# Attention and channel mixing in one kernel: more probability tiles transposed by block transposes and DMAs, the input normalised on GpSimd, and new timetables

## What is computed

```python
xn = layernorm(x)                                  # over the last axis
# attention: 8 query heads of 128, one shared key and value head
q = xn @ Wq + bq + pe;  k, v = split(xn @ Wkv + bkv);  k = k + pe
p = softmax(causal(q @ k.T / sqrt(128)))           # 1024 x 1024 for each head
attn = concat_heads(p @ v) @ Wo
# channel mixing, with the token before (zero for the first)
xr = mu_r * xn + (1 - mu_r) * prev(xn);  xk = mu_k * xn + (1 - mu_k) * prev(xn)
ffn = sigmoid(xr @ W_r) * (relu(xk @ W_k)**2 @ W_v)
out = x + attn + ffn
```

## Time and profile before

| | us |
|---|---|
| median of three runs (1562.58 to 1563.08) | 1562.81 |
| the profiled execution, whole | 1561.37 |
| its span, first to last instruction | 1559.6 |
| PE busy, 12032 matmuls | 1533.5 |
| VectorE, ScalarE, GpSimd busy | 1210.4, 1056.2, 1060.7 |
| mean granted clock of PE | 0.996 |

### The profile page before, as it was taken

The page is one execution under the profiler, slowest core; times in us unless marked ns, Lnnn a source line. Parts: engine busy times, 40 slices in busy tenths (PEclk is TensorE's granted clock), DMA queues, the critical chain, the costliest instruction groups (busy, mean ns, idle before and its releaser), DMA issues.

```text
span 1559.6 us, 35317 instructions
## 1 busy us (share of the span) xinstructions
PE 1533.5 (98%) x12032; PEld 1497.6 (96%) x12032; DVE 1210.4 (78%) x3284; ACT 1056.2 (68%) x2531; POOL 1060.7 (68%) x1549
## 2 busy tenths in 40 slices
PE   5999999999999999999999999999999999999998
PEld 5999999999999999999999999999999999999998
DVE  6888767887678876788768787688876888768875
ACT  5776667766667766677577676676766677666764
POOL 5666776667756777567775676756766577765765
PEclk8999999999999999999999999999999999999999
DMA  4014420244202441024410244103431034300443
GB/s 139 9 53 121 146 75 22 58 122 148 69 15 69 129 143 55 15 75 134 144 42 15 86 141 127 42 15 98 140 129 32 12 112 138 129 20 8 119 147 105
DMA packets 151425, 132.46 MB, mean 85 GB/s; under 512 B 12240, under 2 KB 146512, under 8 KB 151248
## 3 DMA queue, kind: packets, MB, share of 16 engines
q1 hardware_dynamic: 150672, 129.55, 27.0%
q10 hardware_dynamic: 576, 0.66, 0.1%
HBM read 67.25 MB, written 62.91 MB: 83 GB/s over the span
## 4 chain that ended last, share of the span: by engine, by line
PE 76%; POOL 10%; issue 7%; DVE 5%; ACT 1%; DMA 0%; POOLq 0%; DVEq 0%; ACTq 0%
PE pS L893 25%; PE pO L893 23%; PE pG L893 19%; PE pT L986 8%; POOL qt L450 3%; POOL X L506 3%; DVE gate L698 1%; POOL pt L465 1%; POOL mh L456 1%; DVE X L872 1%; POOL rstd L434 1%; DVE mix L742 1%; POOL v L444 1%; POOL X L505 1%; DVE pt L797 1%
## 5 line engine op out<-in xcount | busy, mean ns | idle before, releaser
L893 PE MATMUL pO<-pt,v 128*128 128x256 f32 x3456 | 466.6, 285 | 6.5 <-DVE ot L848 5.3
L893 PE MATMUL pS<-kt,qt 128*128 128x288 f32 (+41 forms) x2304 | 458.6, 329 | 2.0 <-POOL qt L450 2.0
L659 ACT ACTIVATE X<-X,bias 128x16 f32<-128x16 f32 (+56 forms) x512 | 375.9, 734 | 93.3 <-DVE bias L872 92.8
L893 PEld LDWEIGHTS pO<-pt,v 128*128 128x128 f32 x3456 | 426.1, 189 | 12.1 <-DVE ot L848 10.0
L872 DVE CUSTOM_DVE_ANT_0 X<-pS,mask 128x16 f32<-128x16 f32 (+56 forms) x512 | 353.8, 691 | 45.1 <-issue 22.9
L506 POOL TENSOR_SCALAR X<-X,rec 128x16 f32<-128x16 f32 (+56 forms) x512 | 367.0, 717 | 23.0 <-DVE rec L780 23.0
L893 PEld LDWEIGHTS pS<-kt,qt 128*128 128x128 f32 x2304 | 367.5, 190 | 14.0 <-issue 2.2
L465 POOL TENSOR_TENSOR pt<-Z,pt 128x640 fp32r<-128x640 f32 (+3 forms) x128 | 256.6, 2005 | 63.3 <-ACT pt L588 61.6
L797 DVE TENSOR_TENSOR pt<-pT,pt 128x512 fp32r<-128x512 f32 (+3 forms) x512 | 257.3, 522 | 26.6 <-ACT pt L595 23.7
L595 ACT CAST pt<-pT 128x512 fp32r<-128x512 f32 (+3 forms) x512 | 223.0, 461 | 61.7 <-PE pT L986 58.8
L652 ACT CAST ot<-pO 128x256 fp32r<-128x256 f32 x256 | 96.2, 376 | 241.2 <-PE pO L893 115.0
(11 more groups left out here) (101 smaller groups left out, 1788.6 us busy)
## 6 DMA issues: line engine op xcount, KB each, us to landing
park_dram<-Y SPq DMA_DIRECT2D x32, 512.0 KB, 2.6
Z<-park_dram SPq DMA_DIRECT2D x128, 128.0 KB, 2.8
park_dram<-Y SPq DMA_DIRECT2D x32, 448.0 KB, 3.0
Z<-park_dram SPq DMA_DIRECT2D x128, 112.0 KB, 2.5
park_dram<-Y SPq DMA_DIRECT2D x32, 384.0 KB, 2.9
Z<-park_dram SPq DMA_DIRECT2D x128, 96.0 KB, 2.3
park_dram<-Y SPq DMA_DIRECT2D x32, 320.0 KB, 2.7
Z<-park_dram SPq DMA_DIRECT2D x128, 80.0 KB, 2.1
```

Of the source, the lines that this page charges most:

```text
L659: nc.scalar.activation(x_row(s, 0, w), x_row(s, 0, w), ACT.Exp, bias=bias[:, j:j + 1], scale=-1.0, accum_out=total[:, j:j + 1]).then_inc(e ...
L893: last = nc.tensor.matmul(out, a[i], m[j], start=start and k == 0, stop=stop and k == n - 1)
```

## The change

It sets `turned` to the even steps from 16 on: the first step of each pair in rows 2 and 3 of tiles (3 and 4 key tiles) takes the detour too, 24 tiles of a batch row in place of 16. `Y` and `park_dram` get two and four slots, the fetch is split from `park` and issued one turn later, `park` and `fetch` stand ahead of the stores in SP's program. `xnt` and `xt` have one buffer, with waits on ScalarE (`xt_ready`, `prev_ready`, `mix_ready`) ahead of its reuse. `norm_apply` moves from VectorE to GpSimd. On PE, `WO` stands ahead of the other fillers and of the pair's product; on VectorE statistics and `token_mix` stand behind the fillers' evictions; on GpSimd `split_q` and `split_v` stand ahead of the side work. `LEAD` is 10; `TURNS`, `WO_AT`, `AT` and `HALVES` have new entries. The staging of the weights moves to other parts of `X` and `Y`. A path on which ScalarE scales (`scaled_by_act`) is never taken, as no step is over 999, and `H_LAG` for odd steps is not used either. The core of the diff (the other three chunks' entries in `TURNS` are changed in the same way: `FV` of chunks 1 and 2 goes from 12 to 14, `Q` of chunk 1 from 11 to 9, `KT` and `KV` one turn earlier, `FR` of chunk 3 from 5 to 7):

```diff
-H_LAG = 7
-L_LAG = 7
+H_LAG = (7, 6)
+L_LAG = (7, 7)
+C_LAG = 2
 QTMP = 2
-LEAD = 12
+LEAD = 10
...
      (7, "FR", 0, 0),
      (8, "Q", 1, 1),
      (10, "Q", 1, 2),
-     (12, "KV", 1, 0),
+     (11, "KV", 1, 0),
      (13, "Q", 1, 3),
      (14, "FV", 0, 0),
-     (15, "KT", 1, 0)),
+     (14, "KT", 1, 0)),
     ((0, "FK", 0, 0),
      (3, "XT", 1, 0),
      (4, "FR", 0, 0),
      (7, "Q", 1, 0),
      (8, "Q", 1, 1),
-     (11, "Q", 1, 2),
-     (12, "FV", 0, 0),
-     (12, "KV", 1, 0),
+     (9, "Q", 1, 2),
+     (11, "KV", 1, 0),
      (12, "Q", 1, 3),
-     (14, "KT", 1, 0)),
+     (13, "KT", 1, 0),
+     (14, "FV", 0, 0)),
...
-WO_AT = (17, 25, 33, 41, 49, 57, 66, 72)
+WO_AT = (17, 26, 33, 41, 49, 56, 65, 73)
 AT = {"stats": (0, 0, 0, 0),
       "apply": (0, 0, 0, 0),
       "inv": (0, 0, 0, 0),
-      "mixr_prev": (0, 1, 0, 0),
-      "mixr_dve": (1, 1, 1, 1),
+      "mixr_prev": (0, 0, 0, 0),
+      "mixr_dve": (0, 1, 1, 0),
       "mixr_out": (3, 2, 4, 1),
-      "ka_out": (6, 5, 6, 8),
-      "mixk_prev": (5, 7, 6, 7),
-      "mixk_dve": (6, 13, 9, 11),
-      "mixk_out": (8, 14, 13, 13)}
-HALVES = (0, 1, 2, 3, 6, 4, 0, 1, 2, 3, 5, 4, 0, 1, 6, 2, 3, 4, 0, 1, 5, 2, 3, 4, 6, 0, 1, 2, 3, 7, 8, 9)
+      "ka_out": (8, 5, 6, 8),
+      "mixk_prev": (5, 4, 6, 7),
+      "mixk_dve": (9, 12, 11, 10),
+      "mixk_out": (10, 14, 14, 13)}
+HALVES = (1, 7, 6, 9, 8, 5, 1, 7, 6, 9, 8, 5, 1, 7, 6, 9, 8, 5, 1, 7, 8, 9, 1, 5, 8, 7, 1, 9, 4, 6, 5, 8, 0, 2, 4, 6, 0, 8, 4, 2, 0, 6, 4, 8, 0, 2, 4, 6, 0, 8, 4, 2, 0, 6, 4, 8, 0, 2, 4, 6, 0, 8, 4, 2)
...
-    if s < SHARED:
-        return HALVES[s], 1
-    return (s // 2 % 2 * 2, 2) if turned(s) else ((s - SHARED) // 2 % 3 * 2 + 4, 2)
+    return HALVES[s], 1 if s < SHARED else 2
 
 
 def turned(s):
 
-    return s >= SHARED and s % 2 == 0
+    return s >= 16 and s % 2 == 0
+
+
+def zeroed(s):
...
+    return P - (s % H + 1) * SUB
+
+def scaled_by_act(s):
+    return s > 999
...
+        if it >= T_LAG and it - T_LAG < STEPS:
+            order += [(b, ("T", it - T_LAG, m)) for m in range(len(t_banks(it - T_LAG)))]
...
-        xnt = sb("xnt", [P, 2, CT, CHUNK + 1])
-        xt = [sb(f"xt{i}", [P, 2, CT, CHUNK], R) for i in range(2)]
+        xnt = sb("xnt", [P, CT, CHUNK + 1])
+        xt = [sb(f"xt{i}", [P, CT, CHUNK], R) for i in range(2)]
         qt = [sb(f"qt{i}", [P, 2, CHUNK // SUB, H, SUB], R) for i in range(2)]
...
-        Y = sb("Y", [P, 4, NT, 32])
+        Y = sb("Y", [P, 2, 4, NT, 32])
         Z = sb("Z", [P, 2, 4, NT, 32])
...
-            def move(b, s):
-
-                k = turned_no(b, s)
-                slot, nk = k % 2, s // H + 1
+            def park(b, s):
+
+                k, nk = turned_no(b, s), s // H + 1
                 sp.wait_ge(turned_ready, k + 1)
-                if k >= 2:
-                    sp.wait_ge(landed[slot], 64 * (k // 2))
-                sp.dma_start(park_d[slot, :, :, 0:nk * 32],
-                             Y[:, :, 0:nk, :].rearrange("p a k c -> p a (k c)")).then_inc(parked, 16)
+                if k >= 4:
+                    sp.wait_ge(landed[k % 4], 64 * (k // 4))
+                sp.dma_start(park_d[k % 4, :, :, 0:nk * 32],
+                             Y[:, k % 2, :, 0:nk, :].rearrange("p a k c -> p a (k c)")).then_inc(parked[k % 2], 16)
+
+            def fetch(b, s):
+
+                k, nk = turned_no(b, s), s // H + 1
+                sp.wait_ge(parked[k % 2], 16 * (k // 2 + 1))
                 if k >= 2:
                     sp.wait_ge(turned_lo, k - 1)
-                sp.wait_ge(parked, 16 * (k + 1))
                 for q in range(4):
-                    sp.dma_start(Z[32 * q:32 * (q + 1), slot, :, 0:nk, :].rearrange("r a k c -> r a (k c)"),
-                                 park_d[slot, :, q, 0:nk * 32].rearrange("(a r) n -> r a n", a=4)
-                                 ).then_inc(landed[slot], 16)
+                    sp.dma_start(Z[32 * q:32 * (q + 1), k % 2, :, 0:nk, :].rearrange("r a k c -> r a (k c)"),
+                                 park_d[k % 4, :, q, 0:nk * 32].rearrange("(a r) n -> r a n", a=4)
+                                 ).then_inc(landed[k % 4], 16)
 
             for b, it in turns():
+                if it - V_LAG - 1 in TURNED:
+                    fetch(b, it - V_LAG - 1)
+                if it - V_LAG in TURNED:
+                    park(b, it - V_LAG)
                 for r in [r for r in range(NT) if min(WO_AT[r] + 1, LAST_IT - 1) == it]:
                     store(b, r // TPC, r % TPC)
                 for r in [r for r in range(1, NT, TPC) if min(WO_AT[r] + 4, LAST_IT - 1) == it]:
                     if b < B - 1:
                         reload(b, r // TPC)
-                if it - V_LAG in TURNED:
-                    move(b, it - V_LAG)
...
+            def norm_apply(n, slot):
+                pool.wait_ge(rstd_ready, n + 1)
+                for t in range(TPC):
+                    nc.gpsimd.tensor_scalar(xn[:, t, :], xtok[:, slot, t, :], mv[:, t, 0:1], rstd[:, t:t + 1],
+                                            ALU.subtract, ALU.mult).then_inc(xn_ready, 1)
...
+                c, i = it // PER, it % PER
+                if it < STEPS:
+                    if i == AT["inv"][c] and not absent(b, c + 1):
+                        inv_std(chunk_no(b, c + 1))
+                    if i == AT["apply"][c] and not absent(b, c + 1):
+                        if chunk_no(b, c):
+                            pool.wait_ge(mixed, chunk_no(b, c))
+                        norm_apply(chunk_no(b, c + 1), (c + 1) % NC)
+                    if i == AT["mixr_out"][c]:
...
                 act.wait_ge(filled["XT"], n + 1)
+                if n:
+                    act.wait_ge(xt_ready, n)
+                    act.wait_ge(prev_ready, 2 * n * CT)
+                    act.wait_ge(mix_ready, 2 * n * CT)
                 g = g_bank("XT", c, 0).rearrange("p (t n) -> p t n", t=CT)
                 if c % NC:
-
-                    nc.scalar.copy(xnt[:, slot, :, 0:1], xnt[:, 1 - slot, :, CHUNK:CHUNK + 1])
-                nc.scalar.copy(xt[0][:, slot, :, :], g)
-                nc.scalar.copy(xnt[:, slot, :, 1:CHUNK + 1], g).then_inc(xnt_ready, 1)
+                    nc.scalar.copy(xnt[:, :, 0:1], xnt[:, :, CHUNK:CHUNK + 1]).then_inc(last_kept, 1)
+                nc.scalar.copy(xt[0][:, :, :], g)
+                if c % NC:
+                    act.wait_ge(last_kept, n - n // NC)
+                nc.scalar.copy(xnt[:, :, 1:CHUNK + 1], g).then_inc(xnt_ready, 1)
...
-                s = it - H_LAG
-                if s in TURNED:
+                for s in [s for s in TURNED if s + H_LAG[s % 2] == it]:
                     nk = s // H + 1
                     k = turned_no(b, s)
                     if b or s // 2 > 1:
                         act.wait_ge(pv_done, b * (STEPS // 2) + s // 2 - 1)
-                    act.wait_ge(landed[k % 2], 64 * (k // 2 + 1))
-                    nc.scalar.copy(pt_of(0, s, nk), Z[:, k % 2, :, 0:nk, :]).then_inc(turned_hi, 1)
+                    act.wait_ge(landed[k % 4], 64 * (k // 4 + 1))
+                    nc.scalar.copy(pt_of(0, s)[:, 0:nk, :].rearrange("p k (a c) -> p a k c", a=4),
+                                   Z[:, k % 2, :, 0:nk, :]).then_inc(turned_hi, 1)
...
                 dve.wait_ge(bn_done, n * 2 * TPC + TPC)
+                if n:
+                    dve.wait_ge(xn_ready, n * TPC)
                 dve.sem_inc(dve_passed, 1)
                 for t in range(TPC):
                     nc.vector.bn_aggr(mv[:, t, :], stats[:, t, :]).then_inc(bn_done, 1)
                 dve.wait_ge(bn_done, n * 2 * TPC + 2 * TPC)
                 nc.vector.tensor_scalar_add(vare[:, :], mv[:, :, 1], EPS).then_inc(var_ready, 1)
-
-            def norm_apply(n, slot):
-                dve.wait_ge(rstd_ready, n + 1)
-                for t in range(TPC):
-                    nc.vector.scalar_tensor_tensor(xn[:, t, :], xtok[:, slot, t, :], mv[:, t, 0:1],
-                                                   rstd[:, t:t + 1].broadcast_to((P, E)),
-                                                   ALU.subtract, ALU.mult).then_inc(xn_ready, 1)
...
-                    if k:
-                        dve.wait_ge(parked, 16 * k)
-                    nc.vector.transpose(Y[:, :, 0:nk, :].rearrange("p a k c -> p k a c"),
+                    if scaled_by_act(s):
+                        dve.wait_ge(scaled, b * C_FIRST[STEPS] + C_FIRST[s + 1])
+                    if k >= 2:
+                        dve.wait_ge(parked[k % 2], 16 * (k // 2))
+                    nc.vector.transpose(Y[:, k % 2, :, 0:nk, :].rearrange("p a k c -> p k a c"),
...
-                c, i = it // PER, it % PER
-                if it < STEPS:
-                    n = chunk_no(b, c)
-                    if i == AT["stats"][c] and not absent(b, c + 1):
-                        norm_stats(chunk_no(b, c + 1), (c + 1) % NC, b)
-                    if i == AT["apply"][c] and not absent(b, c + 1):
```

(23 more changed lines are left out.)

195 lines of the change are left out of this document (109 added, 86 removed).

## The result

The changed kernel is slower: median 1573.92 us of five runs (1571.56 to 1576.64) against 1562.81 (1562.34 to 1563.24) before; ratio 1.0074, 95% interval [1.0059, 1.0089]. I had forecast 1538.

What follows compares the result with a forecast made beforehand. PE's instruction stream, busy 98% of a 1559.6 us span, was taken as the bound. Less 19.0 (transposes) and 6 (normalisation) gave 1534.6; adding 1.8 around the span and 1.4 to the median gave 1538 us, range 1530 to 1553.

Steps and rivals of the forecast that it cites:

- Point 4: Normalised input moved from VectorE to GpSimd: VectorE earlier, PE's stalls for `ot` shrink; 6 us less, bounds 0 and 10.
- Point 1: 224 fewer transposes on PE, even steps 16 to 30: 19.0 us less, counting in full on the saturated stream.
- Point 2: Detour work on other engines: ScalarE and VectorE about unchanged, GpSimd's subtractions 78 us, under 80% busy, off the path.
- Point 3: Detoured tiles arrive before their product; tightest is step 16, 8.9 us needed of 9.9; cost 0, bound 6 us.
- The sign I named: For the detour's tiles arriving in time: no wait of ScalarE for `Z`, none of PE for GpSimd's `pt`.
- Point 5: Single buffer for `xnt` and `xt`, `WO` order, `LEAD`, `HALVES`, filler places: costed at 0, fillers +/- 4 us.
- (b): VectorE takes over as bound in steps 16 to 37, its block transposes waiting for scaling: 1545 to 1559, chance 0.2.
- the sign I gave for (b): PE waits of over 2 us a row whose releaser is VectorE's mask.
- (c): Slower: detour too long for rows 2 and 3, PE stands at each pair; 1576 us, chance 0.06.

Runs made afterwards that it cites:

- the microbenchmark: The kernel before with fourteen extra GpSimd operations at its start, 128x256 fp32, each form twice, each waiting for the one before; one run, 1571.17 us.
- the timetables alone: The changed kernel with normalisation back on VectorE and the detour from step 32 on only; new timetables, order and single buffers kept: 1559.48 us, 0.9984.
- the first experiment: The changed kernel with `norm_apply` back on VectorE in its old place, everything else as changed: 1560.44 us, 0.9992.

## Why the prediction was wrong

**Point 4 is the step that failed.** It priced the normalisation on GpSimd by its scaling of 272 elements, 0.49 us. That row is right: the same form takes 0.48 in the microbenchmark. But it is another pair of operations, and subtract with multiply takes 1.22. I had bounded the gain of this edit by 0 and 10 us, and put no upper end on the duration itself, though no row of before showed a subtract in such an instruction. The changed kernel against the one with one multiplication says what this was worth: 1.0074 - 0.9889 = 1.85%, 29 us, the clock that fell behind the stalls included. I had a sentence for what is queued behind ("the scaling of step 14 (30, 46, 62), one or two us late for a use four turns on"); that was the tile of an even step, and the same change makes VectorE's block transpose use it one turn on, at the head of an in-order queue. I had priced the two parts one by one, and the loss is where they meet.

**The gain of point 4 was real and too small.** With the old detour, from the timetables alone (1559.48) to a normalisation that VectorE doesn't stand for (1549.98, 1550.08), it is 9.5 us; I took 6, with 10 as the bound.

**Point 1 is wrong twice, in opposite directions.** A transpose is worth 0.11 us by the steps, 24.6 us for 224, and not 19.0: from the first transpose to the first start of the next work it is 0.24 us for three, but that next matmul starts 0.03 us behind the last transpose and the second one behind it comes 0.26 us later where 0.17 is the rule, and this 0.09 belongs to the group. And "lying on the saturated stream, it counts in full" is wrong: about 6 us arrive with both rows (1544.53 from 1549.98; 1543.31 from 1550.08), and 10.3 of 15.3 where no other work is moved. Row 2 brings 7 to 9 of its 96 x 0.11 = 10.5, row 3 nothing of its 128 x 0.11 = 14. The busy share of 98% and the few waits of the earlier trace rows don't show how closely the other engines follow PE: with both rows the table has 0.2 to 0.8 us given back at five steps of a row.

**Point 2** was right on ScalarE and VectorE (block transposes of 0.574 and 0.693 us in the first experiment), and too low on GpSimd only by the normalisation: 41.28 of 51.88 us in the third chunk are 80%.

**Point 3** was right by the medians and wrong for the tile that it named as the tightest. Writes of the tiles with 3 key tiles land after 2.4 us and fetches after 1.9 (below), where I took 2.7 and 2.1. But the write of step 16's tile landed after 4.0 to 4.3 us in five of the eight batch rows of the changed kernel, and in a sixth its fetches were issued late, and PE waited at the product of steps 16 and 17, as shown above: 4.5 us in all at step 24, where I took 0 and bounded it by 6. For the other new tiles it held: PE's one named wait for GpSimd's `pt`, 2.8 us in 7 cases, at most 0.4, is at the product of steps 62 and 63. The sign I named did appear, ScalarE waiting 26.0 us for `Z`; GpSimd's subtraction stands behind ScalarE's copy (72.6 us in all, 61.6 before).

```profile
park_dram<-Y SPq DMA_DIRECT2D x32, 192.0 KB, 2.4
Z<-park_dram SPq DMA_DIRECT2D x128, 48.0 KB, 1.9
```

**Point 5**, costed at 0, gave some 2.5 us (1 to 4 by the interval): the kernel with the timetables alone is at 0.9984.

**The sum again.** 1538, + 29 for the subtract, + 13 for transposes that don't arrive (6 in place of 19), - 6 for the larger gain of point 4 and the timetables, is 1574; measured 1573.9. It closes because each of these terms is a difference between runs; it is bookkeeping and no second proof.

**The rivals.** The mechanism of (b) is the one that came: a block transpose stands for GpSimd's scaling and holds what is behind it. I had put it at 0.75 us a stand, from 27.8 / 37, and let it end at 1559. The longest are 3.3 us, and PE met them at `WO`'s eviction, not at the mask, so the sign I gave for (b), a wait of over 2 us a row for the mask, didn't appear. The slower side, (c), was given 0.06 for a detour that is too long. It is too long for one tile, by 0.4 to 1.3 us in six batch rows, which doesn't make the kernel slower; no case had the normalisation in it.

**The shared interfaces.** I weighed the Trainium skill's rule (GPSIMD Engine Reference, Specifications: GpSimd's SBUF interfaces are shared with VectorE, and VectorE's instructions with two SBUF inputs or in a 2-port perf mode contend) at 4 us off the path. The last section shows that it holds here for `token_mix`, which has two SBUF inputs: 475 ns alone, 1180 beside `pt<-Z`. The normalisation behind the mask has one SBUF input besides its two pointers and lasts longer still, 1631; which mode it runs in, no trace shows. And it was not all off the path: turn 33, 1.0 us of VectorE's time in a row, and step 30, 0.3 us.

What stays open: why the write of one tile lands late in some batch rows, the rest of VectorE's 1.5 us before it normalises, and what lengthens step 38. That row 3 costs what it gives was measured.

## What to carry to other kernels

Price an operation on another engine by a row with the same operations, not only the same shape and name, and where no row has them give its duration an upper end and follow that end through the in-order queue behind it. Ask of every item in that queue who uses it after the change, since the same change may have moved the use closer. Look at single rounds of a loop beside the medians, since a tile that is late in half of them hides there, and look at the granted clock in each. On a stream that is 98% busy, work taken out counts in full only where the engines that take it over have slack in that very step, and a table of step lengths against a base shows where; move it tile by tile.

## What the runs showed of the hardware

GpSimd's `tensor_scalar` on 128x256 fp32 takes 0.40 to 0.56 us with multiplications and additions, and 1.07 to 1.22 us in the three forms whose first operation is a subtract, with constants as with pointers. The Trainium skill, GPSIMD Engine Reference, section "Elementwise — side-by-side cycle accounting", has 1.8 cycles an element at 1.2 GHz as the best case, an estimate of 0.38 us for 256 elements: the 0.40 us of two multiplications with constants agrees with it, and the 1.07 of the same with a subtract is nearly three times that. A subtraction written as mult and add with a negated, scaled shift is the way round, and costs two operations on 128x2 elements.

**VectorE beside GpSimd.** In the kernel that normalises behind the mask, the mean length of VectorE's instructions by what GpSimd did during the largest part of each (ns, number of cases):

| on VectorE | GpSimd idle | scaling of `X` | `pt<-Z` subtraction |
|---|---|---|---|
| `norm_apply`, 256 elements, SBUF only | 406 (26) | 576 (23) | 1631 (15) |
| `token_mix`, 256, SBUF only | 475 (72) | 758 (17) | 1180 (7) |
| `pt<-pT` subtraction, 512, one input in PSUM | 652 (8) | 648 (28) | 666 (134) |

The subtraction with an input in PSUM lasts as long beside either. The two that work in SBUF alone last up to four times as long beside GpSimd's subtraction of two SBUF inputs; `token_mix` took 1008 ns in 16 cases beside another such subtraction, that of `qt`. Block transposes, SBUF to SBUF as well, don't notice it: 841 ns for 640 elements under the subtraction and 831 on average in the kernel with the old detour. With row 2 alone on the detour 7 of the normalisations fall beside such a subtraction, with both rows 15.

**The same write.** 192 KB from `Y` to `park_dram`, the tile of step 16, landed 2.4 us after its issue in four batch rows of that kernel and 3.8 to 4.3 us after it in the other four.
